# One list of steps for five engines, drawn in another order

## The chip, the core and the metric

The kernel runs on one core of a Trainium2 chip. The metric is device time in microseconds; the median of three runs before the change is 268.47 us (265.78 to 269.16). A profile of one execution goes with it.

## The reference

Four batches of 256 tokens of width 256 go through two layers. Layer 0 is attention and an MLP, each with a layer norm whose scale and shift, and a gate (gamma), come from a condition vector. Layer 1 is RMS norm and attention with rotary positions and a mask.

```python
def layer0(x, cond):                      # 16 heads of 16
    gamma1, gamma2, scale1, scale2, shift1, shift2 = split(silu(cond) @ Wada.T + bada)
    q, k, v = heads((ln(x) * (scale1 + 1) + shift1) @ Wqkv.T + qkv_bias)
    p = softmax(q / |q| * sm @ (k / |k|).T + attn_bias)
    x = x + ((p @ v) @ Wproj.T + bproj) * gamma1
    h = gelu_tanh((ln(x) * (scale2 + 1) + shift2) @ Wfc1.T + bfc1)    # width 1024
    return x + (h @ Wfc2.T + bfc2) * gamma2

def layer1(x, cond):                      # 4 heads of 64
    h = rms_norm(x, cond @ norm_w.T + 1)
    q, k, v = heads(h @ qkv_w.T)
    q, k = rope(q * sqrt(scale) / |q|, k * sqrt(scale) / |k|)
    return (softmax(where(mask, q @ k.T, -1e30)) @ v) @ out_w.T + x
```

The projections take their operands in high and low halves, so each is made of three matmuls (L785, L786, L787) where one would do.

## The kernel before

The work is cut into 407 steps such as `qk0:2.1`: a name whose last digit is the layer where there are two, the batch, and within it a tile of 128 tokens or an index of heads. Everything stays on the chip after the loads. `ORDER` is one list of all steps, and PE, DVE, ACT and POOL each walk it: `walk` runs, step by step, the part that belongs to its own engine and skips the rest. So each engine's instructions stand in the order of the list, and no engine overtakes itself. Between engines semaphores wait for the producer of an operand. PE's results go to three PSUM banks in turn, numbered in the list's order; `claim` waits until the user of the bank's last content, three results earlier in the list, has emptied it. SP's loads and stores are a program of their own beside the list.

The steps that are spoken of below. In layer 0, for a batch b: `stats0`, `norm0` (DVE: xh, L1136), `normed0` (PE transposes, ACT makes xmt at L588), `split0` (DVE: xm_hi and xm_lo, L1145 and L1146), `qk0:b.t` (PE L785 to L787, DVE L1256), `unit0`, `hi0` and `lo0` (the normalised q and k in halves), `turnq0` and `turnk0` (PE transposes, ACT copies to qstk at L659 and to kstk at L672 and L673), `max0:b.i` (PE L838, DVE row maxima at L1153, eight per batch and two instructions each), `score0:b.i` (PE L863, ACT exponentials at L598), `value0` (PE L883), `out0`, `heads0` (ACT L605, L606), `heads0_lo` (DVE L1193), `proj0`. `gamma:b` spreads a batch's gate over the partitions (PE L949, ACT L640); `bias_count` (DVE L1223, L1224) looks at the attention bias; `split_wqkv0` and `split_w1` make the halves of weights (ACT L569 the high half, DVE L1105 or POOL L517 the low one). The MLP is `fc1`, `gelu`, `fc2`. In layer 1: `square1` (POOL L536), `rsums1` (DVE L1344), `rope` (DVE L1360 to L1369), `turn1` (PE transposes, ACT L739), `score1:b.t` (PE L1032, L1037), `max1` (DVE L1376), `exp1` (ACT L750), `diag1` (DVE L1382, L1387), `turnp1` (PE L1047, copies on ACT L763 and DVE L1400), `value1` (PE L1062), `heads1`, `heads1_lo` (DVE L1404), `proj1`.

Of the kernel before, what the change touches and what calls it, by code (L numbers as in the profile page):

```python
# [73 lines left out]


ORDER = [(name, *map(int, filter(None, rest.split(".")))) for name, _, rest in (word.partition(":") for word in """
const_sel silu const_v zeros:0 stats0:0 norm0:0 ada split_wqkv0 normed0:0 head_scales split0:0 stats0:1
const_stack square0:0.0 square0:0.1 stats0:2 norm0:1 root0:0 qk0:0.0 qk0:0.1 sums0:0 normed0:1 zeros:1 split0:1
norm0:2 ada_rest stats0:3 v0:0 v0:1 unit0:0.0 unit0:0.1 normed0:2 square0:1.0 qk0:1.0 square0:1.1 root0:1
lo0:0.0 lo0:0.1 qk0:1.1 hi0:0.0 hi0:0.1 bias_count sums0:1 square0:2.0 turnk0:0.0 turnq0:0.0 turnq0:0.1 flag  # L80
split0:2 turnk0:0.1 gamma_rows max0:0.0 v0:2 max0:0.1 norm0:3 gamma:0 gamma:1 gamma:2 gamma:3 hi0:1.0
square0:2.1 hi0:1.1 unit0:1.0 unit0:1.1 max0:0.2 lo0:1.0 lo0:1.1 qk0:2.0 qk0:2.1 max0:0.3 max0:0.4 max0:0.5
turnk0:1.0 normed0:3 sums0:2 max0:0.6 max0:0.7 neg0:0 turnq0:1.0 turnq0:1.1 split0:3 shift0:0 split_wproj
turnk0:1.1 unit0:2.0 unit0:2.1 qk0:3.0 qk0:3.1 max0:1.0 score0:0.0 score0:0.1 max0:1.1 hi0:2.0 score0:0.2
max0:1.2 score0:0.3 max0:1.3 mask hi0:2.1 lo0:2.0 value0:0.0 max0:1.4 score0:0.4 score0:0.5 lo0:2.1 take0:0.0
max0:1.5 value0:0.1 max0:1.6 score0:0.6 score0:0.7 root0:2 max0:1.7 neg0:1 turnq0:2.0 out0:0.0 turnq0:2.1
shift0:1 square0:3.0 sums0:3 turnk0:2.0 turnk0:2.1 value0:0.2 value0:0.3 take0:0.1 max0:2.0 score0:1.0 max0:2.1
score0:1.1 square0:3.1 max0:2.2 score0:1.2 score0:1.3 unit0:3.0 hi0:3.0 max0:2.3 value0:1.0 max0:2.4 score0:1.4
xbias0:0 score0:1.5 unit0:3.1 hi0:3.1 max0:2.5 out0:0.1 value0:1.1 max0:2.6 take0:1.0 score0:1.6 score0:1.7
lo0:3.0 heads0:0 take0:1.1 root0:3 max0:2.7 neg0:2 heads0_lo:0 value0:1.2 value0:1.3 shift0:2 lo0:3.1 turnk0:3.0  # L90
proj0:0 turnq0:3.0 turnq0:3.1 turnk0:3.1 stats1:0 out0:1.0 out0:1.1 score0:2.0 max0:3.0 score0:2.1 max0:3.1
heads0:1 max0:3.2 score0:2.2 max0:3.3 score0:2.3 max0:3.4 score0:2.4 max0:3.5 score0:2.5 xbias1:0 xbias0:1
xbias1:1 heads0_lo:1 max0:3.6 value0:2.0 norm1:0 value0:2.1 max0:3.7 neg0:3 take0:2.0 xbias0:2 score0:2.6
split_w1 v0:3 score0:2.7 shift0:3 proj0:1 stats1:1 value0:2.2 value0:2.3 take0:2.1 score0:3.0 score0:3.1
out0:2.0 out0:2.1 score0:3.2 heads0_lo:2 score0:3.3 heads0:2 value0:3.0 value0:3.1 normed1:0 take0:3.0 norm1:1
xbias1:2 score0:3.4 score0:3.5 proj0:2 stats1:2 score0:3.6 score0:3.7 split_w2 value0:3.2 value0:3.3 split1:0
take0:3.1 out0:3.0 normed1:1 out0:3.1 split1:1 heads0_lo:3 norm1:2 fc1:0.0 xbias0:3 xbias1:3 fc1:0.1 fc1:0.2
heads0:3 fc1:0.3 gelu:0.0 gelu:0.1 gelu:0.2 gelu:0.3 fc1:1.0 fc1:1.1 proj0:3 stats1:3 split1:2 normed1:2 fc1:1.2
fc1:1.3 norm1:3 gelu:1.0 gelu:1.1 gelu:1.2 split_wqkv1 split_wout1 fc2:0 stats2:0 normed1:3 square1:0.0
square1:0.1 norm2:0 gelu:1.3 fc1:2.0 cos:0.0 fc1:2.1 cos:0.1 gelu:2.0 split1:3 fc1:2.2 gelu:2.1 split2:0 fc1:2.3  # L100
normed2:0 gelu:2.2 gelu:2.3 fc2:1 stats2:1 qk1:0.0 qk1:0.1 rsums1:0 norm2:1 fc2:2 root1:0 fc1:3.0 stats2:2
fc1:3.1 gelu:3.0 gelu:3.1 norm2:2 normed2:1 fc1:3.2 split2:1 gelu:3.2 cos:1.0 fc1:3.3 gelu:3.3 rope:0.0 v1:0
rope:0.1 normed2:2 qk1:1.0 square1:1.0 square1:1.1 split2:2 fc2:3 stats2:3 rsums1:1 turn1:0.0 max1:0.0 max1:0.1
qk1:1.1 turn1:0.1 score1:0.0 score1:0.1 norm2:3 exp1:0.0 rope:1.0 rope:1.1 diag1:0.0 v1:1 rsums1:2 qk1:2.0 v1:2
diag1:0.1 qk1:2.1 turn1:1.0 turn1:1.1 max1:1.0 normed2:3 exp1:0.1 turnp1:0.0 score1:1.0 score1:1.1 split2:3
rope:2.0 cos:1.1 turnp1:0.1 exp1:1.0 rope:2.1 qk1:3.0 qk1:3.1 diag1:1.0 max1:1.1 value1:0 turn1:2.0 rsums1:3
diag1:1.1 turn1:2.1 heads1_lo:0 exp1:1.1 root1:1 square1:2.0 square1:2.1 cos:2.0 heads1:0 turnp1:1.0 cos:2.1
score1:2.0 max1:2.0 score1:2.1 max1:2.1 turnp1:1.1 rope:3.0 rope:3.1 diag1:2.0 v1:3 exp1:2.0 value1:1 turn1:3.0
exp1:2.1 proj1:0 diag1:2.1 turn1:3.1 turnp1:2.0 turnp1:2.1 root1:2 heads1:1 heads1_lo:1 square1:3.0 max1:3.0
max1:3.1 diag1:3.0 score1:3.0 score1:3.1 square1:3.1 cos:3.0 value1:2 diag1:3.1 exp1:3.0 exp1:3.1 proj1:1  # L110
heads1_lo:2 heads1:2 turnp1:3.0 turnp1:3.1 root1:3 heads1_lo:3 proj1:2 value1:3 proj1:3 cos:3.1 heads1:3
""".split())]
# [1345 lines left out]
```

How the kernel before makes its waits and increments, by code:

```python
            def step(ins):  # L346
                count[0] += 1
                ins.then_inc(s, 1)
                eng.wait_ge(s, count[0])
# [8 lines left out]
        @block.sync  # L359
# [30 lines left out]
            sp.dma_start(mask_u8, mask.rearrange("b (t p) k -> p b t k", p=P)).then_inc(s_mask, 16)  # L390
            def shift_rows(b):
                sp.wait_ge(*emptied(("shT", b)))
                for par in range(2):
                    sp.dma_start(qstk[SLOT * par + 48:SLOT * par + 50, b % 2, :, :].bitcast(F32),
                                 shs[2 * PAIRS * par:2 * PAIRS * (par + 1), :]).then_inc(shift_in, 16)
            shift_rows(0)
            sp.wait_ge(*full(("gam_rows",)))
            sp.wait_ge(*emptied(("ada2",)))
            sp.dma_start(stage_a[:, 0:FC * HID].rearrange("p (f n) -> p f n", f=FC),
                         wfc1.rearrange("(f p) n -> p f n", p=P)).then_inc(s_w1, 16)
            sp.wait_ge(w_hi, 2)
            sp.wait_ge(w_lo_d, 2)
            sp.dma_start(stage_b[:, :].rearrange("p (f n) -> p f n", f=HC),
                         wfc2.rearrange("(f p) n -> p f n", p=P)).then_inc(s_w2, 16)
            for b in range(1, B):
                shift_rows(b)
            sp.wait_ge(w_hi, 3)
            sp.wait_ge(w_lo_p, 1)
            sp.dma_start(stage_a[:, 0:FC * 3 * C].rearrange("p (f n) -> p f n", f=FC),
                         wqkv1.rearrange("(f p) n -> p f n", p=P)).then_inc(s_wq1, 16)
            sp.wait_ge(w_hi, 4)
            sp.wait_ge(w_lo_p, 2)
```

## Time and profile before

| | before |
|---|---|
| median of 3 runs, us | 268.47 (265.78 to 269.16) |
| profiled execution, span, us | 266.0 |
| PE busy, us | 232.5 (87%) |
| DVE busy, us | 202.7 (76%) |
| ACT busy, us | 154.9 (58%) |
| POOL busy, us | 117.4 (44%) |
| mean granted clock of TensorE | 0.987 |

The profiled execution's own time is its span, 266.0 us from the first to the last instruction; it is 2.5 us shorter than the median of the runs. Seen by stage, 0 to 143 us is layer 0's attention, 143 to 199 the MLP, and 199 to 266 layer 1. A row of a timeline gives the start, the length, the engine and line, what is written from what, the number of instructions joined in it, and in brackets how long the engine stood idle ahead of it and what ended that.

### The profile page before, as it was taken

To read this page: it belongs to the slowest core of one execution; us is meant where nothing else is said; L and a number is where in the kernel's file an instruction comes from. 1 tells how busy PE (TensorE), PEld (TensorE's weight loads), DVE (VectorE), ACT (ScalarE), POOL (GpSimd) and SP (SyncE) were. 2 spreads that over 40 slices of the span, in tenths; PEclk is the share of its full clock that TensorE was granted. 3 is DMA by queue.
4 is the path that set the end of the run, shared out by engine and by line. 5 is a ranking of instruction groups with operands and counts; after the bars stand their busy time and mean duration, and the time that the engine had idled before them with its cause. 6 is when DMAs were issued, how large, how long until landed. Compare 5 with 4: busy or idle time off the path is not lost.

```text
span 266.0 us, 4823 instructions
## 1 busy us (share of the span) xinstructions
PE 232.5 (87%) x1710; PEld 186.4 (70%) x1710; DVE 202.7 (76%) x421; ACT 154.9 (58%) x303; POOL 117.4 (44%) x184
## 2 busy tenths in 40 slices
...
DMA packets 8248, 10.11 MB, mean 38 GB/s; under 512 B 1824, under 2 KB 7072, under 8 KB 8224
## 3 DMA queue, kind: packets, MB, share of 16 engines
...
q8 instruction: 15, 0.25, 0.4%
q14 instruction: 9, 0.07, 0.1%
...
## 4 chain that ended last, share of the span: by engine, by line
PE 51%; DVE 16%; ACT 11%; issue 8%; POOL 7%; DMA 3%; SPq 2%; ACTq 0%; DVEq 0%; POOLq 0%
PE ring L785 8%; PE ring L786 7%; PE ring L787 7%; PE ring L791 6%; PE ring L838 5%; PE psx L863 5%; PE pv L883 4%; DMA xs<-in_x 3%; PE ring L1047 3%; DVE nm L1153 3%; ACT kstk L673 3%; ACT kstk L672 2%; PE pv L1062 2%; ACT ps L598 2%; POOL nt L450 1%
## 5 line engine op out<-in xcount | busy, mean ns | idle before, releaser
L1153 DVE TENSOR_REDUCE nm<-ring 128x2 f32<-128x512 f32 x64 | 40.2, 683 | 5.3 <-PE ring L838 5.2
L598 ACT ACTIVATE ps<-psx 128x1024 f32<-128x1024 f32 x32 | 31.3, 1026 | 7.5 <-PE psx L863 4.3
L838 PE MATMUL ring<-kstk,qstk 128*128 128x512 f32 x64 | 25.0, 449 | 4.1 <-ACT kstk L673 2.7
L785 PE MATMUL ring<-wqkv_hi,xm_hi 128*128 128x512 f32 (+1 forms) x64 | 24.3, 379 | 4.4 <-DVE xm_lo L1146 2.9
L786 PE MATMUL ring<-wqkv_lo,xm_hi 128*128 128x512 f32 (+1 forms) x64 | 23.3, 364 | 0.0
L787 PE MATMUL ring<-wqkv_hi,xm_lo 128*128 128x512 f32 (+1 forms) x64 | 22.9, 358 | 0.0
L838 PEld LDWEIGHTS ring<-kstk,qstk 128*128 128x128 f32 x64 | 11.3, 193 | 13.9 <-DVE nm L1153 5.3
L791 PE MATMUL ring<-ident,stack 128*128 128x128 f32 x128 | 17.7, 278 | 2.9 <-ACT kstk L673 1.4
L863 PE MATMUL psx<-qstk,kstk 128*128 128x256 f32 x128 | 19.7, 287 | 0.3 <-ACT ps L598 0.3
L863 PEld LDWEIGHTS psx<-qstk,kstk 128*128 128x128 f32 x128 | 17.8, 189 | 2.5 <-ACT ps L598 0.9
L883 PE MATMUL pv<-ps,vs 128*32 128x256 f32 x256 | 16.1, 383 | 3.6 <-issue 3.3
L441 POOL TENSOR_TENSOR rstd<-ve,half_neg 128x2 f32<-128x2 f32 x12 | 9.3, 775 | 21.4 <-DVE ve L1122 20.3
L791 PEld LDWEIGHTS ring<-ident,stack 128*128 128x128 f32 x128 | 13.7, 141 | 7.0 <-issue 4.2
L785 PE MATMUL ring<-xm_hi,kstk 128*128 128x256 f32 x64 | 18.5, 289 | 0.1
L702 ACT ACTIVATE ps<-ring,col 128x256 f32<-128x256 f32 x32 | 13.2, 474 | 9.0 <-PE ring L787 8.8
L785 PEld LDWEIGHTS ring<-wqkv_hi,xm_hi 128*128 128x128 f32 x64 | 13.1, 205 | 7.6 <-issue 5.7
L588 ACT ACTIVATE xmt<-ring,mod 128x256 f32<-128x256 f32 x16 | 8.2, 561 | 17.5 <-PE ring L791 17.5
L750 ACT ACTIVATE ps<-psx,nm 128x256 f32<-128x256 f32 x32 | 14.7, 484 | 6.2 <-DVE nm L1376 6.2
L787 PE MATMUL ring<-xm_hi,kstk 128*128 128x256 f32 x64 | 18.1, 283 | 0.0
L786 PE MATMUL ring<-xm_lo,kstk 128*128 128x256 f32 x64 | 18.1, 283 | 0.0
L536 POOL TENSOR_TENSOR qn<-qk 128x512 f32<-128x512 f32 x8 | 9.1, 1142 | 20.0 <-ACT qk L724 15.2
L488 POOL TENSOR_TENSOR qn<-qk 128x512 f32<-128x512 f32 x8 | 8.3, 1042 | 20.9 <-DVE qk L1256 10.7
...
## 6 DMA issues: line engine op xcount, KB each, us to landing
...
```

Of the source, the lines that this page charges most:

```text
L441: g.tensor_tensor(rstd[:, kind, b, :], ve[:, kind, b, :], half_neg[:, 0:TB], ALU.pow)\
L598: a.activation(ps[:, n % 4], psx[:, n % 2], ACT.Exp).then_inc(exp_done, 1)
L702: last = a.activation(gelu_u[:, n % 4, i * L:(i + 1) * L], bank(key)[:, i * L:(i + 1) * L], ACT.Gelu_apprx_tanh, bias=col[:, 16 + 2 * i_ + ...
L750: ins = a.activation(weights_q[m % 2][:, i, f, :], psx[:, n % 2, i, f, :], ACT.Exp, bias=nm1[:, m % 2, 2 * i + f:2 * i + f + 1], accum_out ...
L785: mm(dst, lhs[0], rhs[0], start=start, stop=False)
L786: mm(dst, lhs[0], rhs[1], start=False, stop=False)
L787: return mm(dst, lhs[1], rhs[0], start=False, stop=stop)
L791: last = nc.tensor.transpose(dst[:, i * P:(i + 1) * P], src, ident[:, :])
L838: last = mm(dst, qstk[:, b % 2, p, qc * P:(qc + 1) * P], kstk[:, b % 2, 2 * p:2 * p + 2, :], start=True, stop=not with_bias)
L863: last = mm(dst[:, i, kc, :], kstk[:, b % 2, 2 * p + i, keys], qstk[:, b % 2, p, :], start=True, stop=not with_bias)
L883: last = mm(pv[32 * i:32 * i + 32, cols_], vs[:, b % 3, kc, 4 * g + i, :], ps[:, slot, i % 2, kc, :], start=(kc == 0), stop=(kc == TB - 1))
L1153: v.tensor_reduce(nm[:, qc, :, p], bank(key).rearrange("p (h n) -> p h n", h=2), AX.X, ALU.max, negate=True).then_inc(ring_dve, 1)
```

## The change

Only `ORDER` is redrawn. It holds the same 407 steps, with the same instructions, buffers, waits and loads; what differs is where each step stands, and with it which result gets which PSUM bank. The diff replaces all lines of the list; the lines of the two places with a shift on DVE below are these.

```diff
@@ -74,41 +74,42 @@
-const_sel silu const_v zeros:0 stats0:0 norm0:0 ada split_wqkv0 normed0:0 head_scales split0:0 stats0:1
-const_stack square0:0.0 square0:0.1 stats0:2 norm0:1 root0:0 qk0:0.0 qk0:0.1 sums0:0 normed0:1 zeros:1 split0:1
...
-diag1:0.1 qk1:2.1 turn1:1.0 turn1:1.1 max1:1.0 normed2:3 exp1:0.1 turnp1:0.0 score1:1.0 score1:1.1 split2:3
-rope:2.0 cos:1.1 turnp1:0.1 exp1:1.0 rope:2.1 qk1:3.0 qk1:3.1 diag1:1.0 max1:1.1 value1:0 turn1:2.0 rsums1:3
-diag1:1.1 turn1:2.1 heads1_lo:0 exp1:1.1 root1:1 square1:2.0 square1:2.1 cos:2.0 heads1:0 turnp1:1.0 cos:2.1
...
+const_sel const_v zeros:0 silu stats0:0 split_wqkv0 norm0:0 head_scales ada const_stack split0:0 stats0:1
+normed0:0 square0:0.0 qk0:0.0 square0:0.1 stats0:2 norm0:1 qk0:0.1 root0:0 sums0:0 normed0:1 split0:1 ada_rest
...
+root1:2 cos:2.1 split2:3 max1:1.0 max1:1.1 normed2:3 score1:1.0 score1:1.1 turnp1:0.0 turnp1:0.1 rope:2.0
+rope:2.1 exp1:1.0 exp1:1.1 diag1:1.0 rsums1:3 max1:2.0 diag1:1.1 qk1:3.0 qk1:3.1 value1:0 max1:2.1 turn1:2.0
+turn1:2.1 score1:2.0 score1:2.1 heads1:0 heads1_lo:0 turnp1:1.0 turnp1:1.1 exp1:2.0 exp1:2.1 rope:3.0 v1:3
...
```

The first place is DVE near the start: `split_wqkv0` (wqkv_lo) and `norm0:0` (xh). Before:

```order
L1122 TENSOR_SCALAR ve<-mv 128x2
L1136 TENSOR_SCALAR xh<-xs,mv,rstd 128x256 x2
L1092 TENSOR_TENSOR mod<-ring,col 128x8 x2
L1100 TENSOR_SCALAR mod<-mod 128x8
L1105 TENSOR_TENSOR wqkv_lo<-stage_b,wqkv_hi 128x1536
L1213 TENSOR_SCALAR sm<-row 128x16
L1145 CAST xm_hi<-xmt 128x512
L1146 TENSOR_TENSOR xm_lo<-xmt,xm_hi 128x512
```

and in the changed list:

```order
L1123 TENSOR_SCALAR ve<-mv 128x2
L1106 TENSOR_TENSOR wqkv_lo<-stage_b,wqkv_hi 128x1536
L1137 TENSOR_SCALAR xh<-xs,mv,rstd 128x256 x2
L1214 TENSOR_SCALAR sm<-row 128x16
L1093 TENSOR_TENSOR mod<-ring,col 128x8 x2
L1101 TENSOR_SCALAR mod<-mod 128x8
L1146 CAST xm_hi<-xmt 128x512
L1147 TENSOR_TENSOR xm_lo<-xmt,xm_hi 128x512
```

The low half of wqkv now stands ahead of xh. (Line numbers of the changed kernel are higher by one.)

The second place is ACT between batch 1's and batch 2's exponentials. kstk is written in `turnk0`, qstk in `turnq0`, o_raw in `take0`. Before:

```order
L673 ACTIVATE kstk<-ring 64x4x128
L618 ACTIVATE o_raw<-pv 128x512
L598 ACTIVATE ps<-psx 128x1024 x4
L649 ACTIVATE stack<-qn 128x32x16
L650 ACTIVATE stack<-qn 128x16x16
L651 ACTIVATE stack<-qn 128x16x16
L598 ACTIVATE ps<-psx 128x1024 x2
```

and in the changed list, where gam is `gamma:3`:

```order
L674 ACTIVATE kstk<-ring 64x4x128
L660 ACTIVATE qstk<-ring 128x4x128 x4
L619 ACTIVATE o_raw<-pv 128x512
L599 ACTIVATE ps<-psx 128x1024 x3
L641 ACTIVATE gam<-ring 128x512
L599 ACTIVATE ps<-psx 128x1024
L650 ACTIVATE stack<-qn 128x32x16
L651 ACTIVATE stack<-qn 128x16x16
L652 ACTIVATE stack<-qn 128x16x16
```

The copies of q now follow those of k, where they stood ahead of them, and the gate of batch 3 is spread between two exponentials of batch 2.

The third place is DVE in layer 1, from the rope of batch 2's second tile on; nm is `max1`, ss is `rsums1:3`, inv and o_raw are `diag1:1.0`. Before:

```order
L1400 COPY ps<-ring 128x4x128
L1360 TENSOR_TENSOR stage_a<-qk,rope_sb 128x512
L1365 TENSOR_TENSOR qn<-stage_a 128x8x32
L1366 TENSOR_TENSOR qn<-stage_a 128x8x32
L1369 TENSOR_TENSOR qn<-qn,rn 128x512
L1382 RECIPROCAL inv<-sums 128x4
L1387 TENSOR_TENSOR o_raw<-ident,inv 128x512
L1376 TENSOR_REDUCE nm<-psx 128x4
L1344 TENSOR_REDUCE ss<-qn 128x8 x2
L1348 TENSOR_SCALAR ss<-ss 128x2x8
L1112 TENSOR_SCALAR nt<-ss 128x2x8
L1113 TENSOR_SCALAR rn<-nt 128x2x8
```

and in the changed list:

```order
L1361 TENSOR_TENSOR stage_a<-qk,rope_sb 128x512
L1366 TENSOR_TENSOR qn<-stage_a 128x8x32
L1367 TENSOR_TENSOR qn<-stage_a 128x8x32
L1370 TENSOR_TENSOR qn<-qn,rn 128x512
L1383 RECIPROCAL inv<-sums 128x4
L1388 TENSOR_TENSOR o_raw<-ident,inv 128x512
L1345 TENSOR_REDUCE ss<-qn 128x8 x2
L1349 TENSOR_SCALAR ss<-ss 128x2x8
L1113 TENSOR_SCALAR nt<-ss 128x2x8
L1114 TENSOR_SCALAR rn<-nt 128x2x8
L1377 TENSOR_REDUCE nm<-psx 128x4
```

The maximum that stood between the diagonal and the sums of squares is gone from there (it stands ahead of the ropes of batch 2), and the next maximum comes after the sums.

Four more moves are spoken of. On PE, `score1:3.0` comes directly behind `turn1:3.1`, where `turnp1:2.0` and `turnp1:2.1` stood between; `qk0:2.0` and `qk0:2.1` come ahead of `max0:0.0`; the four `gamma` steps, which stood in a row, are spread from `max0:0.5` to `score0:1.2`. On POOL `split_w1` comes ahead of `xbias0:2` (L504, L505), which it followed. On ACT `normed1:0` comes ahead of batch 3's first exponential.

## Rows read from the trace of the kernel before

**Rows 1.** Windows: length, busy us of PE, PEld, DVE, ACT, POOL; granted clock; DMA.

```profile
46.00:53.00 7.00, 7.00 (x18) 4.93 (x17) 4.39 (x9) 3.56 (x9) 1.04 (x1) 0.51 0.00 0
...
143.00:199.00 56.00, 55.91 (x453) 54.97 (x452) 42.40 (x87) 32.86 (x69) 23.18 (x29) 1.00 0.02 6
199.00:266.00 67.00, 58.69 (x424) 45.16 (x422) 52.21 (x92) 32.36 (x95) 25.03 (x51) 1.00 0.05 17
```

**Rows 2.** Timeline of DVE at the start.

```profile
10.47 0.74 DVE L1136 TENSOR_SCALAR xh<-xs,mv,rstd 128x256 f32<-128x256 f32 x2 [4.43 <-POOL rstd L441]
...
11.94 1.75 DVE L1105 TENSOR_TENSOR wqkv_lo<-stage_b,wqkv_hi 128x1536 fp32r<-128x1536 f32 x1
...
13.69 0.41 DVE L1145 CAST xm_hi<-xmt 128x512 fp32r<-128x512 f32 x1
...
16.24 0.89 DVE L1118 BATCH_NORM_STATS2 bnst<-xs 128x6 f32<-128x256 f32 x2 [1.41 <-DMA xs<-in_x]
```

**Rows 3.** Timeline of ACT and PE at the start.

```profile
9.71 1.48 ACT L569 ACTIVATE wqkv_hi<-stage_b 128x1536 fp32r<-128x1536 f32 x1 [6.91 <-DMA stage_b<-in_wqkv]
12.42 1.02 ACT L588 ACTIVATE xmt<-ring,mod 128x256 f32<-128x256 f32 x2 [1.23 <-PE ring L791]
...
14.97 0.77 PE L785 MATMUL ring<-wqkv_hi,xm_hi 128*128 128x512 f32 x1 [2.60 <-DVE xm_lo L1146]
```

**Rows 4.** Groups of instructions: busy us, mean ns of one, idle before and its releasers.

```profile
L1153 DVE TENSOR_REDUCE nm<-ring 128x2 f32<-128x512 f32 x64 | 40.2, 683 | 5.3 <-PE ring L838 5.2
L598 ACT ACTIVATE ps<-psx 128x1024 f32<-128x1024 f32 x32 | 31.3, 1026 | 7.5 <-PE psx L863 4.3
```

**Rows 5.** DVE, PE and ACT from 33 to 54 us, with the window before the clock's fall.

```profile
33.86 0.69 DVE L1224 TENSOR_SCALAR_CACHE_REDUCE o_raw<-bias_sb 128x512 f32<-128x512 f32 x1
...
46.28 0.62 PE L949 MATMUL ring<-at_lo,sel 8*128 8x512 f32 x1
...
46.94 0.60 ACT L640 ACTIVATE gam<-ring 128x512 f32<-128x512 f32 x1 [0.24 <-PE ring L949]
...
50.66 0.69 DVE L1256 TENSOR_TENSOR qk<-ring,row 128x512 f32<-128x512 f32 x1 [0.36 <-PE ring L787]
53.10 0.69 DVE L1256 TENSOR_TENSOR qk<-ring,row 128x512 f32<-128x512 f32 x1 [1.75 <-PE ring L787]
...
44.00:46.00 2.00, 1.82 (x7) 1.14 (x8) 2.00 (x6) 1.09 (x2) 0.00 (x0) 0.99 0.00 0
```

**Rows 6.** DVE at the turn from batch 1 to batch 2.

```profile
87.81 3.68 DVE L1153 TENSOR_REDUCE nm<-ring 128x2 f32<-128x512 f32 x6 [3.86 <-PE ring L838]
```

**Rows 7.** ACT, DVE and POOL from 117 to 134 us; last, at_lo's durations (min/median/max).

```profile
117.94 1.94 ACT L598 ACTIVATE ps<-psx 128x1024 f32<-128x1024 f32 x2 [3.03 <-PE pv L883]
...
131.22 2.46 DVE L1193 TENSOR_TENSOR at_lo<-stage_a,at_hi 128x512 fp32r<-128x512 f32 x1 [2.22 <-ACT at_hi L606]
...
128.56 4.57 POOL L517 TENSOR_TENSOR kstk<-stage_a,kstk 128x2048 fp32r<-128x2048 f32 x1
...
L1193 DVE TENSOR_TENSOR at_lo<-stage_a,at_hi x4: 679/692/2460, 100.5 to 149.7; 128x512 fp32r<-128x512 f32 x4
```

**Rows 8.** PE before and at the start of the MLP.

```profile
133.82 0.36 PE L785 MATMUL ring<-wp_hi,at_hi 128*128 128x256 f32 x1 [0.65 <-DVE at_lo L1193]
...
143.26 0.36 PE L785 MATMUL ring<-xm_hi,kstk 128*128 128x256 f32 x1
```

**Rows 9.** DVE and POOL in layer 1, around the sums of batch 3.

```profile
227.85 1.22 DVE L1376 TENSOR_REDUCE nm<-psx 128x4 f32<-128x1024 f32 x1
...
229.99 0.69 DVE L1344 TENSOR_REDUCE ss<-qn 128x8 f32<-128x512 f32 x1 [0.31 <-POOL qn L536]
...
227.83 2.04 POOL L536 TENSOR_TENSOR qn<-qk 128x512 f32<-128x512 f32 x2 [4.23 <-ACT qk L724]
```

**Rows 10.** ACT and PE behind the last turn of layer 1.

```profile
242.18 0.62 ACT L739 ACTIVATE vs<-ring 128x512 f32<-128x512 f32 x1
...
242.12 3.81 PE L1047 MATMUL ring<-o_raw,ps 128*128 128x128 f32 x32
```

More of the change, by code:

```diff
@@ L76 @@
 ORDER = [(name, *map(int, filter(None, rest.split(".")))) for name, _, rest in (word.partition(":") for word in """
-const_sel silu const_v zeros:0 stats0:0 norm0:0 ada split_wqkv0 normed0:0 head_scales split0:0 stats0:1
-const_stack square0:0.0 square0:0.1 stats0:2 norm0:1 root0:0 qk0:0.0 qk0:0.1 sums0:0 normed0:1 zeros:1 split0:1
-norm0:2 ada_rest stats0:3 v0:0 v0:1 unit0:0.0 unit0:0.1 normed0:2 square0:1.0 qk0:1.0 square0:1.1 root0:1
-lo0:0.0 lo0:0.1 qk0:1.1 hi0:0.0 hi0:0.1 bias_count sums0:1 square0:2.0 turnk0:0.0 turnq0:0.0 turnq0:0.1 flag
@@ L81 @@
[L81 to L104, printed above, removed]
-diag1:0.1 qk1:2.1 turn1:1.0 turn1:1.1 max1:1.0 normed2:3 exp1:0.1 turnp1:0.0 score1:1.0 score1:1.1 split2:3
@@ L106 @@
-rope:2.0 cos:1.1 turnp1:0.1 exp1:1.0 rope:2.1 qk1:3.0 qk1:3.1 diag1:1.0 max1:1.1 value1:0 turn1:2.0 rsums1:3
-diag1:1.1 turn1:2.1 heads1_lo:0 exp1:1.1 root1:1 square1:2.0 square1:2.1 cos:2.0 heads1:0 turnp1:1.0 cos:2.1
-score1:2.0 max1:2.0 score1:2.1 max1:2.1 turnp1:1.1 rope:3.0 rope:3.1 diag1:2.0 v1:3 exp1:2.0 value1:1 turn1:3.0
-exp1:2.1 proj1:0 diag1:2.1 turn1:3.1 turnp1:2.0 turnp1:2.1 root1:2 heads1:1 heads1_lo:1 square1:3.0 max1:3.0
-max1:3.1 diag1:3.0 score1:3.0 score1:3.1 square1:3.1 cos:3.0 value1:2 diag1:3.1 exp1:3.0 exp1:3.1 proj1:1
@@ L111 @@
-heads1_lo:2 heads1:2 turnp1:3.0 turnp1:3.1 root1:3 heads1_lo:3 proj1:2 value1:3 proj1:3 cos:3.1 heads1:3
+const_sel const_v zeros:0 silu stats0:0 split_wqkv0 norm0:0 head_scales ada const_stack split0:0 stats0:1
+normed0:0 square0:0.0 qk0:0.0 square0:0.1 stats0:2 norm0:1 qk0:0.1 root0:0 sums0:0 normed0:1 split0:1 ada_rest
+norm0:2 stats0:3 v0:0 bias_count v0:1 unit0:0.0 unit0:0.1 normed0:2 qk0:1.0 square0:1.0 square0:1.1 root0:1
+lo0:0.0 square0:2.0 qk0:1.1 lo0:0.1 hi0:0.0 hi0:0.1 turnk0:0.0 zeros:1 sums0:1 turnq0:0.0 turnq0:0.1 norm0:3
@@ new lines @@
+flag split0:2 turnk0:0.1 gamma_rows v0:2 unit0:1.0 unit0:1.1 normed0:3 qk0:2.0 square0:2.1 lo0:1.0 qk0:2.1
+max0:0.0 max0:0.1 hi0:1.0 hi0:1.1 max0:0.2 max0:0.3 lo0:1.1 turnk0:1.0 sums0:2 turnk0:1.1 root0:2 max0:0.4
+max0:0.5 gamma:0 max0:0.6 max0:0.7 unit0:2.0 square0:3.0 mask turnq0:1.0 turnq0:1.1 square0:3.1 gamma:1 neg0:0
+unit0:2.1 hi0:2.0 shift0:0 max0:1.0 gamma:2 hi0:2.1 max0:1.1 max0:1.2 xbias0:0 score0:0.0 max0:1.3 score0:0.1
+max0:1.4 score0:0.2 score0:0.3 value0:0.0 split0:3 max0:1.5 score0:0.4 score0:0.5 lo0:2.0 max0:1.6 value0:0.1
```

24 lines of the change are left out of this document (added).

## The prediction

> **What bounds the kernel now.** I read three views. First the windows by stage, because each stage has its own limit [rows 1]. In the MLP (143 to 199 us) PE is busy 55.91 of 56.00 us: only an earlier or later start can move that stage. In layer 1 (199 to 266) no engine is full, PE 58.69 and DVE 52.21 of 67; the attention of layer 0 ahead of the MLP is of the same kind. What sets the time there is the order, since an engine that waits holds everything behind it. Second, the instructions one by one where the list differs; third, group rows for durations [rows 4].
>
> No instruction is added or removed, so the sum is made of waits alone: those of before that the new order fills, and those that it opens. I followed the new list engine by engine with the durations of before and noted how much later the same instruction comes. Terms that overlap don't add up, so each term below is the change of one running delay. The delay counts at two points: the first fc1 matmul, before at 143.26 [rows 8], since PE is full from there on, and the last scores.
>
> **1. Start, +2.3.** Before, DVE makes xh as soon as rstd is there (10.47, 0.74 long) and splits wqkv (11.94, 1.75) while PE transposes xh and ACT makes xmt (12.42, 1.02) [rows 2, 3]. Now the split stands ahead of xh. It needs ACT's high half, which runs from 9.71 to 11.19 [rows 3], so it ends near 11.19 + 1.75 = 12.94, and xh near 13.7, where it ended at 11.21. From xh's end to xmt's end it took 2.23 (11.21 to 13.44), from the cast's start to the first qk product 1.28 (13.69 to 14.97) [rows 2, 3]: 13.7 + 2.23 + 1.28 = 17.2 to 17.3 with a handover, +2.3. The floor is zero if something later waits for a DMA anyway: the statistics of batch 1 waited for their x till 16.24 [rows 2]. But they feed batch 1, and the first product leads the chain of batch 0, so I take the full 2.3.
>
> **2. 18 to 56 us, running +1.0.** On DVE bias_count (a reduction of 0.69 [rows 5] and a shorter instruction) is moved ahead of batch 0's values and of batch 1's second qk tile: +0.8. Against it: PE's granted clock was 0.51, the 1.2 GHz level, from 46 to 53 us [rows 1]. It fell as PE ran the four gamma steps in a row (the last matmul at 46.28, 0.62 long), and DVE then waited 0.36 and 1.75 us for qk0:2.0 and qk0:2.1 at half pace, 2.1 in the middle of its row of maxima [rows 5]. The new list spreads the gammas over the next stages and runs qk0:2.x ahead of the maxima. I take it that the clock stays up, and the 2.1 comes back: 2.3 + 0.8 - 2.1 = 1.0. The Trainium skill (TensorE: Matmul & The Clock Gate, "What's actually happening") lets the clock fall after the array has idled. The trace doesn't bear that out, for PE was busy 1.82 of the 2.00 us up to the fall [rows 5]; so I go by what ran. By the page, spreading the gammas would save nothing of itself, and the sum would be 2.1 higher.
>
> **3. Batches 1 to 3, 56 to 111 us, running +2.1.** The pace is DVE's 64 maxima of 0.683 us with ACT's 32 exponentials of 1.026 beside them [rows 4]. At the turn to batch 2 DVE waits 3.86 us for ACT's copies of k, ahead of the maxima [rows 6]. The new order puts q's copies behind k's; the maxima need both, so the same copies stand in line and the wait stays, less 0.1. Then gamma:3 (0.60 [rows 5]) is put between exponentials where ACT has no gap, and proj0:0 (twelve matmuls; such a step's first is at 133.82 [rows 8]) ahead of the k turn of batch 3: +1.2 together. Bounds: 0 if ACT's other waits swallow them, and about 2.3 (twice my value) if they also push a row of maxima.
>
> **4. 111 to 143 us, running +1.85.** value0:2.0 is taken earlier, which fills ACT's wait of 3.03 us at 117.94 [rows 7]; but the maxima on DVE go on meanwhile, so I count none of it. heads0_lo:2 took 2.46 us where the other three take 0.68 to 0.69; it ended at 133.68, 0.55 after POOL's 4.57 us split of w1 (128.56 to 133.13) [rows 7], and PE's projection waited for it [rows 8]. Now the split stands further ahead of it, by two POOL instructions that it followed: -1.8 at most, -1.2 after what PE does next. The other way, on ACT normed1:0 (two instructions, 1.02 as at 12.42 [rows 3]) comes ahead of score0:3.0, of which I count +0.7, and handovers +0.25. 2.1 + 0.7 + 0.25 - 1.2 = 1.85. The Trainium skill (SBUF — State Buffer, "Who interferes with whom") says that a DVE instruction with two SBUF inputs is held by a POOL instruction that reads SBUF until that one ends. The two ends, 0.55 us apart, agree. By the rule the gain hangs on POOL's split ending first; if it doesn't, the sum is 1.2 higher.
>
> **5. MLP, +0.15.** PE is full [rows 1], so the delay passes through. The second normalisation of batch 0 and some gelu steps change places: between 0 and 0.3.
>
> **6. Layer 1, +2.0.** (a) Before, max1:1.1 (1.22 at 227.85) filled DVE's time while POOL squared batch 3's q and k (2.04 from 227.83), and rsums1:3 waited only 0.31 [rows 9]. That maximum now stands ahead of the ropes of batch 2, and nothing fills: between 0 and 1.22, I take 0.75. (b) score1:3.0 now directly follows turn1:3.1 on PE, whose result ACT first copies (0.62 from 242.18); before, PE could start turnp1:2 at 242.12 and work on for 3.81 us [rows 10]. PE idles until 242.8 and a handover: between 0.7 and 0.9, I take 0.9. (c) score1:1.1 is ahead of turnp1:0.x, which delays qk1:3.x; mostly hidden under the ropes, 0.35 (bounds 0 and 1.22, its maximum's length). Sum 2.0, bounds 0 (the fillers replace one another) and 3.3. The tail from the last scores keeps its order.
>
> **Sum**: 1.85 + 0.15 + 2.0 = +4.0 us on a profiled span of 266.0. That execution lies near the fast end of the three runs, 2.5 under their median; 266.0 + 4.0 = 270.0 and 268.47 + 4.0 = 272.5. I forecast 271.5, nearer the second.
>
> **Rivals.** *The clock falls again* (chance 0.22). For it: batch 2's products still lie near 45 to 50 us, now ahead of all maxima, where nothing covers them. Against: the gammas are spread. Then the 2.1 isn't regained: 268.47 + 4.0 + 2.1 = 274.6, slower. *The filled waits are real gains* (0.14), the case on the other side. Mechanism: ACT, not DVE, paces 111 to 143, so the 3.03 at 117.94 comes off the MLP's start in full, and the stretched instruction's 1.8 too (0.6 more than counted). It decides if the last exponentials of batch 2 then follow one another without a gap. With it 4.0 - 3.0 - 0.6 = +0.4; with the 2.0 of layer 1 absorbed by the 8.3 us that PE is idle there, -1.6; and if the new order of copies also hides the 3.86, -5.5: 263 to 269. *The delays are absorbed* (0.24): the 2.3 of the start dies at the first wait that doesn't hang on batch 0, and layer 1's fillers replace each other: 0 to +1.5, 268.5 to 270. That the list isn't what runs is excluded: all engines walk it.
>
> **Numbers.** My forecast has the remaining 0.40 and the range 269.5 to 274 of its own. 2% of 268.47, about what a measurement of this kernel can tell from no change, is 5.4: faster is below 263.1, slower above 273.8. Faster 0.13: the far end of the gains' case (0.07), and 0.06 for waits that such a walk doesn't see. Slower 0.35: most of the clock's case (0.18), a fifth of my own (0.08), 0.09 for the upper bounds of terms 3 and 6. Within: 0.52. The range of 264.5 to 276.5 leaves out only the far end of the gains, and the clock's fall together with upper bounds.
>
> **What would show it.** Right: first qk product at 17.3; no fall of the clock before the maxima; fc1 near 145.1; a wait over 1 us ahead of rsums1:3; PE idle ahead of score1:3.0. Wrong: fc1 at or before 143.3, or from fc1 to the end no longer than the 122.7 us of before.

## The result and the profile after

The changed kernel takes 276.64 us (median of 4 runs, 275.61 to 278.42), the kernel before beside it 268.63; the ratio is 1.0325 (95% interval 1.0278 to 1.0373): 8 us slower, where 3 were forecast and 276.5 was the end of the range. The profiled span is 273.7 us against 266.0, +7.7. That execution took 275.61 by the clock of the runs, so some 1.9 us lie around the span.

The same instruction's start, before and after, shows where the 7.7 come from. All are starts on PE.

| | before | after | late by |
|---|---|---|---|
| first qk product | 14.97 | 17.38 | 2.41 |
| shift0:0 | 63.44 | 66.63 | 3.19 |
| max0:2.0 | 87.23 | 89.94 | 2.71 |
| max0:3.0 | 108.83 | 112.11 | 3.28 |
| score0:3.0 | 125.64 | 128.70 | 3.06 |
| score0:3.7, the last score | 135.80 | 137.45 | 1.65 |
| fc1:0.0 | 143.26 | 148.74 | 5.48 |
| fc2:3 | 193.22 | 198.97 | 5.75 |
| proj1:3 | 261.02 | 268.77 | 7.75 |

So 1.65 had been lost at the last scores, 3.83 more went between them and fc1, 0.27 in the MLP and 2.00 in layer 1. The biggest piece lies in a stretch of 8 us to which the prediction gave nothing.

The start first, DVE and PE after (columns as in [rows 2, 3]):

```profile
11.39 1.76 DVE L1106 TENSOR_TENSOR wqkv_lo<-stage_b,wqkv_hi 128x1536 fp32r<-128x1536 f32 x1 [5.35 <-ACT wqkv_hi L570]
13.07 0.73 DVE L1137 TENSOR_SCALAR xh<-xs,mv,rstd 128x256 f32<-128x256 f32 x2
```

```profile
17.38 0.77 PE L786 MATMUL ring<-wqkv_hi,xm_hi 128*128 128x512 f32 x1 [2.41 <-DVE xm_lo L1147]
```

The split runs when its high half is there, xh follows it, and the first product comes at 17.38, as worked out from [rows 2, 3].

Where [rows 5] had DVE wait for qk0:2.x at half clock, the changed kernel has the clock down later. PE there, in the middle of batch 0's maxima, and two windows (columns as in [rows 1], the granted clock third from the end):

```profile
57.38 0.50 PE L839 MATMUL ring<-kstk,qstk 128*128 128x512 f32 x1 [0.72 <-ACT kstk L674]
58.60 1.22 PE L839 MATMUL ring<-kstk,qstk 128*128 128x512 f32 x2 [0.72 <-ACT kstk L674]
```

```profile
56.00:58.00 2.00, 1.00 (x2) 0.37 (x2) 1.50 (x6) 1.93 (x5) 0.83 (x3) 1.00 0.00 0
...
60.00:62.00 2.00, 2.00 (x5) 1.03 (x5) 0.99 (x3) 0.60 (x1) 1.46 (x5) 0.50 0.00 0
```

PE was busy half of the time (1.00 of 2.00 us) before it fell. The delay, 3.19 at shift0:0, is about halved by the last scores, in part because PE no longer waits 0.65 [rows 8] for heads0_lo:2, 0.69 us where [rows 7] had 2.46:

```profile
134.31 0.69 DVE L1194 TENSOR_TENSOR at_lo<-stage_a,at_hi 128x512 fp32r<-128x512 f32 x1 [2.87 <-ACT at_hi L607]
```

Now PE around the last scores. First the kernel before, which the rows ahead of the prediction did not show here, then the changed one:

```profile
135.32 1.12 PE L863 MATMUL psx<-qstk,kstk 128*128 128x256 f32 x8
139.77 1.93 PE L883 MATMUL pv<-ps,vs 128*32 128x256 f32 x32 [3.33 <-issue]
141.64 0.66 PE L791 MATMUL ring<-ident,o_raw 128*128 128x128 f32 x4
```

```profile
136.97 1.12 PE L864 MATMUL psx<-qstk,kstk 128*128 128x256 f32 x8
140.90 1.93 PE L884 MATMUL pv<-ps,vs 128*32 128x256 f32 x14 [2.81 <-issue]
144.00 1.01 PE L884 MATMUL pv<-ps,vs 128*32 128x256 f32 x2 [1.17 <-issue]
144.94 1.12 PE L792 MATMUL ring<-ident,o_raw 128*128 128x128 f32 x4
145.99 1.55 PE L884 MATMUL pv<-ps,vs 128*32 128x256 f32 x16
```

"issue" is time for which the profile shows no wait. Before, PE stands once for 3.33 us and then does 32 matmuls in 1.93. After, it stands for 2.81, does 14, and stands again for 1.17; around this second stop it works at half pace, for the 14 take the 1.93 that 32 took. The windows after show the clock:

```profile
138.00:140.00 2.00, 0.09 (x1) 0.00 (x0) 1.86 (x5) 1.59 (x2) 1.20 (x1) 1.00 0.09 31
140.00:142.00 2.00, 1.10 (x11) 0.68 (x15) 1.22 (x4) 0.00 (x0) 1.69 (x4) 0.55 0.03 8
142.00:144.00 2.00, 0.83 (x7) 0.00 (x0) 0.00 (x0) 0.00 (x0) 1.21 (x1) 0.50 0.00 0
144.00:146.00 2.00, 2.00 (x8) 0.86 (x8) 0.00 (x0) 0.00 (x0) 0.00 (x0) 0.50 0.00 0
146.00:148.00 2.00, 2.00 (x21) 1.00 (x20) 0.75 (x3) 0.39 (x1) 0.00 (x0) 0.75 0.00 0
```

It falls to 0.50, the 1.2 GHz level, while PE stands, and comes back at 147. Before, the same window views from 136 to 144 read 1.00 throughout, though its one stop was longer than either of these. What is at this place in the code: PE alone has two branches on a flag (attention bias zero or not) from the first maximum to the last score. The first is taken, the second jumped over, and both meet behind the last score.

```python
with nc.tensor.If(bias_flag == 0):
    walk(ORDER[FIRST_SCORE:AFTER_SCORES], False)
with nc.tensor.If(bias_flag != 0):
    walk(ORDER[FIRST_SCORE:AFTER_SCORES], True)
walk(ORDER[AFTER_SCORES:], False)
```

Last, layer 1 after: the sums of batch 3 (DVE), and PE ahead of score1:3.0.

```profile
235.49 0.69 DVE L1345 TENSOR_REDUCE ss<-qn 128x8 f32<-128x512 f32 x1 [1.01 <-POOL qn L537]
236.49 0.69 DVE L1345 TENSOR_REDUCE ss<-qn 128x8 f32<-128x512 f32 x1 [0.31 <-POOL qn L537]
```

```profile
249.76 0.59 PE L1033 MATMUL psx<-mask_add,ident_b 128*128 128x512 bf16 x2 [0.73 <-issue]
```

Both waits that the prediction named are there, 1.01 + 0.31 where [rows 9] had 0.31, and 0.73.

### The profile page after: what moved, and what is told of

It reads as the page before. It is cut to its first block, busy times and chain, and to the rows that moved or that the text cites. A ratio compares the mean times of both kernels' runs of the same rounds, so it can differ in the third digit from the quotient of the medians.

```text
span 273.7 us, 4822 instructions
## 1 busy us (share of the span) xinstructions
PE 237.8 (87%) x1710; PEld 188.4 (69%) x1710; DVE 208.3 (76%) x421; ACT 154.4 (56%) x303; POOL 115.5 (42%) x184
## 4 chain that ended last, share of the span: by engine, by line
PE 61%; DVE 13%; ACT 11%; issue 6%; DMA 4%; POOL 2%; SPq 1%; ACTq 0%; DVEq 0%
PE ring L786 8%; PE ring L788 8%; PE ring L787 8%; PE ring L792 7%; PE pv L884 6%; PE ring L839 6%; PE ring L1048 6%; PE psx L864 5%; PE pv L1063 3%; DMA stage_b<-in_wqkv 3%; ACT ps L599 3%; ACT kstk L673 2%; ACT kstk L674 2%; PE psx L1038 2%; DMA qstk<-stage_a 2%
## 5 line engine op out<-in xcount | busy, mean ns | idle before, releaser
L839 PE MATMUL ring<-kstk,qstk 128*128 128x512 f32 x64 | 26.9, 479 | 3.1 <-ACT kstk L674 2.0
L884 PE MATMUL pv<-ps,vs 128*32 128x256 f32 x256 | 18.9, 408 | 4.0 <-issue 4.0
L864 PE MATMUL psx<-qstk,kstk 128*128 128x256 f32 x128 | 20.4, 289 | 1.1 <-ACT ps L599 0.5
L792 PE MATMUL ring<-ident,stack 128*128 128x128 f32 x128 | 18.7, 298 | 2.9 <-ACT kstk L674 1.6
L792 PEld LDWEIGHTS ring<-ident,stack 128*128 128x128 f32 x128 | 15.8, 155 | 5.8 <-issue 4.0
```

Source lines behind the costliest of these rows:

```text
L792: last = nc.tensor.transpose(dst[:, i * P:(i + 1) * P], src, ident[:, :])
L839: last = mm(dst, qstk[:, b % 2, p, qc * P:(qc + 1) * P], kstk[:, b % 2, 2 * p:2 * p + 2, :], start=True, stop=not with_bias)
L864: last = mm(dst[:, i, kc, :], kstk[:, b % 2, 2 * p + i, keys], qstk[:, b % 2, p, :], start=True, stop=not with_bias)
L884: last = mm(pv[32 * i:32 * i + 32, cols_], vs[:, b % 3, kc, 4 * g + i, :], ps[:, slot, i % 2, kc, :], start=(kc == 0), stop=(kc == TB - 1))
```

## The experiments

Two theories for the 3.83 us. **A**: they are PE's stall where the branches meet, and the clock's fall in it. **B**: the new order of the steps behind the last scores waits for something that the profile shows as issue. The runs are e1 to e13; "one branch" means that both branches reach to the end of the program.

**e1 and e2: the branches meet behind everything.** The same edit on the list of before (e1) and on the changed one (e2):

```diff
 with nc.tensor.If(bias_flag == 0):
-    walk(ORDER[FIRST_SCORE:AFTER_SCORES], False)
+    walk(ORDER[FIRST_SCORE:], False)
 with nc.tensor.If(bias_flag != 0):
-    walk(ORDER[FIRST_SCORE:AFTER_SCORES], True)
-walk(ORDER[AFTER_SCORES:], False)
+    walk(ORDER[FIRST_SCORE:], True)
```

> List of before; PE's two branches on the bias flag reach to the end of the program, so they meet behind PE's last instruction and not behind the last scores. Theory A (what was lost between the last scores and fc1 is PE's stall where the branches meet, with the clock that falls in it): the 3.33 us gap at 136.44 is gone, value0:3.2 follows the exponentials (137.94), fc1 starts near 141.4, about 1.9 earlier, and the span is near 264. Theory B (the new order of the steps behind the last scores is what costs): the gap is a wait that shows as issue, and nothing changes: span 266 +- 0.7.

> The changed list with the same edit. Theory A: the gaps of 2.81 and 1.17 and the half clock from 140.2 to 147.1 are gone; fc1, 10.65 us behind the end of score0:3.7 in the changed kernel, comes about 5 behind it; 273.7 goes to about 268, and what is left against before with the same edit is the 1.65 of the attention and the 2.0 of layer 1, about 3.7. Theory B: the changed kernel keeps fc1 at +3.8 against before; 273.7 +- 1.

Measured: e1 265.92 us (span 264.0), ratio to before 0.9905 (0.9876 to 0.9935); e2 269.54 (span 267.5), 1.0047 (1.0018 to 1.0077). PE in e2, the same place:

```profile
136.87 1.12 PE L864 MATMUL psx<-qstk,kstk 128*128 128x256 f32 x8
137.92 1.07 PE L884 MATMUL pv<-ps,vs 128*32 128x256 f32 x16
138.92 0.66 PE L792 MATMUL ring<-ident,o_raw 128*128 128x128 f32 x4
139.54 1.07 PE L884 MATMUL pv<-ps,vs 128*32 128x256 f32 x16
```

The stops are gone and the clock stays up there. From the last score's start to fc1 it takes 4.95 in e1 and 4.67 in e2 (7.46 before, 11.29 after): the new order is, if anything, the shorter one there. B falls. The meeting point costs 2.5 us with the list of before and 6.6 with the changed one; without it the lists differ by 3.6 us instead of 8.

**e3: one step of the start moved back.**

```diff
-... stats0:0 split_wqkv0 norm0:0 head_scales ada const_stack ...
+... stats0:0 norm0:0 head_scales ada split_wqkv0 const_stack ...
```

> The changed list with one step moved back: split_wqkv0 stands behind norm0:0 and ada again. My account: the first qk product comes 2.4 us earlier, at 15.0; rival: that is lost again before the first maxima, or the clock's falls shift, and the end moves by less than 1. By my running delay (1.65 at the last scores, of which 2.4 came from the start) the end comes 1 to 2.4 earlier: 271.3 to 272.7.

275.18 us (span 272.0), in the median 1.5 under the changed kernel, though the runs overlap (273.67 to 278.96 against 275.61 to 278.42). But the edit did not do what it was meant to: the first qk product is at 16.80, not 15.0. ACT shows why.

```profile
12.21 0.22 ACT L630 ACTIVATE sm<-sm 128x16 f32<-128x16 f32 x1 [9.46 <-DVE sm L1214]
12.33 1.47 ACT L570 ACTIVATE wqkv_hi<-stage_b 128x1536 fp32r<-128x1536 f32 x1
```

The high half now stands behind head_scales, which waits through DVE for a load (rows land at 12.0). One delay took the place of the other; e7 does it properly.

**e4: layer 1 in the order of before.** Behind fc2:3 both lists hold the same 97 steps, so that part can be exchanged whole.

```diff
 <changed list up to fc2:3>
-<97 steps, changed order>
+<97 steps, order of before>
```

> The changed list up to fc2:3, and behind it the 97 steps of layer 1 in the order of before (the same steps stand there in both lists). My account: fc2:3 stays 5.7 late and the 2.0 us that layer 1 added are gone: from fc2:3's start to the end 72.8 as before, in place of 74.7; the span is 271.7. Rival (the delay of layer 1 came from the state in which it is entered, not from its order): still 74.7.

275.09 us, in the median 1.5 under the changed kernel; here too the runs overlap (273.11 to 276.51). The stage says it more sharply than the total: from fc2:3 to proj1:3 67.79 us (201.59 to 269.38), in before 67.80, in the changed kernel 69.80. My expectation counted to the program's end; the difference is the same 2.0. The span itself was 274.3, since the meeting point cost more in this execution (12.32 from the last score to fc1).

**e5 and e6: the code shifted, nothing executed changed.** The changed kernel's second stop came behind exactly 14 matmuls. The moved steps qk0:2.x, v0:2 and normed0:3 stand ahead of the branches now, once in the code and not twice, so the meeting point lies some 60 PE instructions earlier by my count. Padding the branch that is not taken moves it. (That 120 of these waits make 60 instructions, and 392 make 196, is my count too.)

```diff
 with nc.tensor.If(bias_flag != 0):
+    for _ in range(120):          # e5, changed list: 60 instructions; e6, list of before: range(392), 196
+        pe.wait_ge(const_ready, 1)
     walk(ORDER[FIRST_SCORE:AFTER_SCORES], True)
```

> The changed list; the branch that PE doesn't take is made 60 instructions longer, nothing that is executed changes. In the changed kernel PE stopped a second time (1.17 us) 14 matmuls behind the point where the branches meet, in before it did not. Theory A1 (the second stop is the fetch of the next block of instructions, and where it lies depends on where the meeting point lies in its block; by my count the changed list moves that point by 60 instructions, since qk0:2.x, v0:2 and normed0:3 now stand once ahead of the branches instead of in both): the stop behind 14 matmuls is gone, as in before; -1.2, and the half clock that followed shortens too: fc1 comes 2 to 4 us earlier, span 270 to 272. Rival A2 (the order behind the scores, value0:3.2, out0:3.0, value0:3.3, makes the stop): it stays behind 14 matmuls, 273.7.

> The list of before; the branch not taken is made 196 instructions longer, which by the same count puts the meeting point where the changed list has it. A1: a second stop of about 1.2 appears some 14 matmuls behind it, and the clock may fall there; fc1 1.2 to 4 later, span 267 to 270. A2: nothing changes, 266.0 +- 0.7.

PE in e5, then in e6:

```profile
136.94 1.12 PE L864 MATMUL psx<-qstk,kstk 128*128 128x256 f32 x8
141.30 1.93 PE L884 MATMUL pv<-ps,vs 128*32 128x256 f32 x16 [3.23 <-issue]
143.16 1.12 PE L792 MATMUL ring<-ident,o_raw 128*128 128x128 f32 x4
```

```profile
133.89 1.12 PE L863 MATMUL psx<-qstk,kstk 128*128 128x256 f32 x8
138.21 1.06 PE L883 MATMUL pv<-ps,vs 128*32 128x256 f32 x14 [3.21 <-issue]
141.41 2.72 PE L883 MATMUL pv<-ps,vs 128*32 128x256 f32 x18 [2.14 <-issue]
```

The second stop has gone from the one and come to the other, behind 14 matmuls again. e3 and e4, whose edits leave the meeting point where the changed list has it, stop a second time behind 14 too (0.90 and 1.44 us). So its place hangs on where the code lies and not on what is executed, as A1 has it.

That PE fetches code there can be read from the traces, in their DMA packets of the kind "instruction", 16 KiB each (times in us):

| | PE stops | packet | PE goes on | next packet | PE stops again |
|---|---|---|---|---|---|
| before | 136.44 | 137.09 to 138.07 | 139.77 | 140.32 to 141.39 | no |
| after | 138.09 | 138.24 to 139.31 | 140.90 | 141.46 to 142.51 | 142.83 to 144.00 |
| e5 | 138.07 | 138.19 to 139.59 | 141.30 | 141.85 to 142.91 | no |
| e6 | 135.00 | 135.57 to 136.63 | 138.21 | 138.77 to 140.10 | 139.27 to 141.41 |

One packet starts within 0.7 us of the beginning of each first stop, the next some 0.55 us behind its end; PE goes on 1.3 to 1.7 us after a packet has landed. Where PE stops again, its work had run out before the second packet landed (e6) or 0.3 us behind that (after). In e1 and e2 no such packet moves between the last scores and fc1. That these packets are PE's, and that the work between the stops is the rest of the first one, is inferred from these times.

e6 takes 271.96 us, ratio to before 1.0143 (1.0106 to 1.0179): before's own list loses 3.5 us by code that never runs. From the last score to fc1 it takes 4.60 longer, 2.14 of it the second stop and the rest with the clock, which stayed up in the first stop and fell at 139.5, in the second. (This execution reached the last score 1.4 earlier than the profiled one of before.) The six runs of e5 lie between 270.6 and 275.3; the ratio to before is 1.0150 (1.0089 to 1.0211), where the changed kernel's was 1.0325, so the stop's going is a gain. The profiled one (span 273.4, expected were 270 to 272) had the clock down from 140 to 147 all the same. Its mean granted clock is 0.956, that of the two fastest runs 0.980 and 0.981: by that difference they had some 13 us less at the half clock (an estimate), in which places isn't shown.

The Trainium skill (Runtime: NRT & Kernel Launch, "Instruction fetch mechanics") says that code is fetched ahead in sequence only, in blocks of 256 instructions, and that a taken branch to a place that isn't at hand waits for its block. The rows agree: a stop and a packet behind each jump. That 196 instructions more bring in the stop that 60 fewer had brought fits blocks of that length too, for the two shifts differ by 256.

**e7 and e8: the start, then also layer 1, of before, on one branch.**

```diff
-... stats0:0 split_wqkv0 norm0:0 head_scales ada const_stack split0:0 stats0:1 normed0:0 ...
+... stats0:0 norm0:0 ada split_wqkv0 normed0:0 head_scales const_stack split0:0 stats0:1 ...   # e7; e8 also e4's edit
```

> The changed list with the branches that reach to the end, and the whole start of before: split_wqkv0 behind norm0:0 and ada, and head_scales behind normed0:0 (in the run with split_wqkv0 alone ACT's high half waited behind head_scales till 12.33). First qk product at 15.0 in place of 16.7. If the start's delay lives on to the end, 267.5 - 1.7 = 265.8; if it is absorbed before the MLP, 267.5 +- 0.5.

> The same with the 97 steps of layer 1 in the order of before. Layer 1's 2.0 are gone as in the run with layer 1 alone: 2.0 under the run before it, near 263.8 to 265.5. If it is under 264.0 it beats the kernel of before with the same branches, so the middle of the new list is a gain there.

e7 has its first product at 14.75 and takes 267.36 us (span 265.6), 2.2 less than e2: the start's delay lives on to the end. (2.0 of it stand in the trace: 16.73 to 14.75. The one run of each with the same high granted clock, 0.987, took 267.43 and 265.38, 2.05 apart.) e8 takes 265.12, another 2.2 less, ratio to before 0.9877 (0.9836 to 0.9918): it lies under both kernels (span 263.6, just under the 264.0 named). Against e1, the list of before with the same branches, it is 0.8 us ahead; the runs overlap (263.93 to 266.44 against 265.23 to 266.15), so the middle of the new list is no clear gain.

**e9: POOL's split earlier, on e1.** heads0_lo:2 took 2.47 us in e1 beside POOL's split of w1, 0.69 in the changed list, where the split ends just ahead of it.

```diff
-... xbias0:2 score0:2.6 split_w1 ... proj0:1 stats1:1 value0:2.2 ...
+... score0:2.6 split_w1 ... proj0:1 stats1:1 xbias0:2 value0:2.2 ...
```

> The list of before with the branches that reach to the end, and one step moved: xbias0:2 behind stats1:1, so that POOL's split of w1 (4.58, in that kernel from 128.99 to 133.57) starts some 2 us earlier and ends before heads0_lo:2. If that DVE instruction took 2.47 there because it had to wait for POOL's, it takes 0.69 now, the projection of batch 2 and fc1 come 1.2 to 1.8 earlier, 264.0 - 1.2 = 262.8 or less, median near 264.5. If its length has nothing to do with POOL, it stays at 2.47 and the time at 264.0.

270.36 us, 4.4 slower than e1, the opposite of both. heads0_lo:2 did come down to 0.69 us. But (DVE, then POOL):

```profile
126.64 4.56 DVE L1121 TENSOR_SCALAR ve<-mv 128x2 f32<-128x2 f32 x1
...
135.15 0.69 DVE L1192 TENSOR_TENSOR at_lo<-stage_a,at_hi 128x512 fp32r<-128x512 f32 x1 [2.38 <-ACT at_hi L606]
```

```profile
126.63 4.55 POOL L517 TENSOR_TENSOR kstk<-stage_a,kstk 128x2048 fp32r<-128x2048 f32 x1
```

An instruction on two elements per partition, 0.17 us elsewhere, took 4.56 and ended within 0.02 of POOL's split. Everything behind it on DVE waited, PE stood, and its clock fell to 0.50 from 132 to 138. So POOL's long instruction does hold DVE here, and not only instructions with two operands in SBUF. The changed kernel has such rows as well, in its MLP, where PE stayed busy. DVE, then POOL:

```profile
150.78 5.05 DVE L1137 TENSOR_SCALAR xh<-x,mv,rstd 128x256 f32<-128x256 f32 x2
```

```profile
151.06 4.62 POOL L522 TENSOR_TENSOR kstk<-stage_b,kstk 128x2048 fp32r<-128x2048 f32 x1 [7.85 <-ACT kstk L570]
```

Such a pair took 0.73 at the start (13.07 above). Moving POOL's split chooses which DVE instruction is hit: in e9 a costly one, in the changed kernel none beside split_w1 (129.69 to 134.27) and this one beside split_w2. The Trainium skill (SBUF — State Buffer, "Who interferes with whom") says that tensor_scalar, too, can need the ports that POOL holds, when its operands allow. These rows agree.

**e10 to e12: pieces of layer 1, on e7.**

```diff
-... max1:1.0 max1:1.1 ... diag1:1.0 rsums1:3 ... turn1:2.1 score1:2.0 ...      # e10 (exp1:1.1 moves too)
+... max1:1.0 ... diag1:1.0 max1:1.1 rsums1:3 ... turn1:2.1 exp1:1.1 score1:2.0 ...
-... heads1:1 score1:3.0 max1:3.0 cos:3.0 heads1_lo:1 turnp1:2.0 turnp1:2.1 max1:3.1 ...   # e11
+... heads1:1 cos:3.0 heads1_lo:1 turnp1:2.0 turnp1:2.1 score1:3.0 max1:3.0 max1:3.1 ...
-... score1:1.0 score1:1.1 turnp1:0.0 turnp1:0.1 ...                              # e12: e10 and this
+... turnp1:0.0 score1:1.0 score1:1.1 turnp1:0.1 ...
```

> The changed list with the start of before and the branches that reach to the end; in layer 1 max1:1.1 is put back behind diag1:1.0 (and exp1:1.1, which needs it, behind turn1:2.1). From fc2:3's start to proj1:3's it took 69.80 with the changed list where the clock didn't fall in it (before 67.80). My terms: the filled wait ahead of rsums1:3 is worth 0.75 of the 2.0: 69.0, and the wait ahead of rsums1:3 is at 0.3 again. Rival: all of the 2.0 hangs on it: 67.8.

> The same base; in layer 1 score1:3.0 is put back behind turnp1:2.1 and max1:3.0 ahead of max1:3.1. My term: 0.9 of the 2.0, so 68.9 from fc2:3's start to proj1:3's, and PE doesn't idle behind turn1:3.1. Rival: PE's 0.73 there is made up elsewhere, 69.8.

> The changed list with the start of before and the branches that reach to the end; in layer 1 max1:1.1 and exp1:1.1 are put back as in the run with the maximum alone, and turnp1:0.0 goes ahead of score1:1.0 on PE and DVE as in before. With the maximum alone nothing was gained: DVE waited 0.77 and 1.09 ahead of the two copies of turnp1:0 instead, since PE does score1:1.1 first. If these two moves belong together, the stretch from turn1:2.1 to score1:3.1 on PE comes down from 21.2 towards 19.8 and the one before it (fc2:3 to turn1:2.1) from 34.84 towards 34.3 where the clock stays up: some 1.2 in all. Rival: both stay, and what layer 1 lost hangs on later steps.

From turn1:2.1 to score1:3.1 on PE it took 19.84 us before, 21.22 after, 21.35 in e10, 20.85 in e11 and 22.11 in e12. So score1:3.0 is worth 0.4, and the maximum nothing: in e10 the wait ahead of the sums is back at 0.28, but DVE waits 0.77 and 1.09 for PE ahead of the two copies of turnp1:0. e12 removed the first of these and lost 0.9 further on. The whole stage from fc2:3 to proj1:3, which the expectations name, took 70.62 in e10, where the clock fell in it (211 to 215), 69.45 in e11 and 70.54 in e12. The medians (267.38, 266.94 and 266.92 against e7's 267.36) tell none of the three apart from e7. Only the whole order gives the 2.0 back (e4, e8).

**e13: the stop without its second half, 2 us earlier.** e7's list with the branches that meet behind the scores, and e5's padding.

> The changed list with the start of before, PE's branches meeting behind the last scores as in the changed kernel, and the branch not taken 60 instructions longer. The second stop is gone as in the run with the shift alone. If the clock falls in the first stop again (it did in every profile of the changed list, and not in before), fc1 comes some 9.5 to 10 behind score0:3.7's start: span 271; if it doesn't, 7.5: span 268.5. A spread of the runs of 2 to 4 us between these two says that the fall is a matter of the single execution.

272.23 us (270.64 to 273.60; span 269.8), 4.9 more than e7. The stop is 3.09 us, the only one; the clock falls at 139.7, 0.4 behind its end, and is back at 143, and fc1 comes 9.17 behind the last score's start, a little under the expected 9.5 to 10. The spread of the runs is 3.0 us (270.64 at a mean clock of 0.975, 273.60 at 0.950), within the 2 to 4 that the expectation took as a sign that the fall varies between executions. In the profiles, one stop with a fall costs 4.5 (9.17 against e2's 4.67; e5 has 5.3), one without a fall 2.5 (before against e1), and two with a fall 6.6 (after against e2).

| | stops, us | clock fell | last score to fc1, us |
|---|---|---|---|
| e2, changed list, one branch | none | no | 4.67 |
| before | 3.33 | no | 7.46 |
| e13 | 3.09 | yes | 9.17 |
| e5 | 3.23 | yes | 9.95 |
| after | 2.81, 1.17 | yes | 11.29 |
| e3 | 3.05, 0.90 | yes | 11.51 |
| e6, list of before | 3.21, 2.14 | yes, in the second | 12.06 |
| e4 | 2.83, 1.44 | yes | 12.32 |

What stays open: why the clock stayed up in the stop of 3.33 us before and in e6's of 3.21, and fell in or just behind the five shorter ones. One execution was profiled of each. The granted clock of the other runs says that executions differ: of the 17 of before beside e1, the six at 0.987, the profile's value, took 266.1 to 268.4 us, the eight at 0.974 or 0.968 took 268.2 to 269.4. Those spent some 7 to 10 us more at the half clock (an estimate from that difference); whether it was in the stop isn't shown.

## Why the prediction was wrong

**The step that failed** is one that was not taken. Between terms 4 and 5 the walk went from the last scores to fc1 at the durations of before, the 3.33 us stall of the kernel before included as it stood, and counted nothing for it. The list doesn't say how PE's code lies in memory, and I treated the order as the only thing that a new order changes. It also sets what stands ahead of the branches and what in both, and with that where they meet in the code. The runs show that the 3.83 us lie at this meeting point (without it the stretch takes 4.67 in e2 and 4.95 in e1), and that PE waits there for code. The shift of the meeting point, 60 instructions by my count, gave the second stop of 1.17 us, with the half clock around it worth 1.3 (11.29 against e5's 9.95) to 2.1 (against e13's 9.17). The rest, 1.7 to 2.5, is the clock's fall at the first stop, which the profiled execution of before didn't have; what decides on it stays open.

**Term by term.** Term 1, 2.3: measured 2.41, and e7 shows that it reaches the end. Term 2, running 1.0: 3.19 at shift0:0. The clock did not stay up; instead of once for 6.8 us it fell from 28 to 31, from 51 to 55 and from 58 to 65, the last time while PE did one or two matmuls at a time between waits of 0.52 to 0.72 us for ACT's copies. So spreading the gammas did not keep it up, and "I go by what ran" was one place read as a rule. Here PE was idle half of the time ahead of the fall; the Trainium skill (TensorE: Matmul & The Clock Gate, "What's actually happening"), which ties the fall to idleness, fits this place better than [rows 5]. It doesn't fit the first fall, at 27.55: PE was busy throughout from 24 to 27.5, the first 2.3 us of it on matmuls of 4 columns. Term 3, running 2.1: 3.28. Term 4, running 1.85: 1.65, near by luck: the loss in terms 2 and 3 was 1.2 larger, and 1.4 came back around batch 2's projection (3.06 at score0:3.0, 1.65 at score0:3.7). Of that, 0.65 is PE's wait for heads0_lo:2, which is gone; [rows 8] shows no more than this, so the term's 1.2 for it was too much. Most of the rest is eight transposes (out0:2.0 and normed1:0) that now stand ahead of score0:3.0. Term 5, 0.15: 0.27. Term 6, 2.0: 2.00 measured and 2.0 in e4. But of its parts only (b) was confirmed, at 0.4 and not 0.9; the filled wait (a) is real as a wait and worth nothing by itself. Its division was wrong, so the 2.0 was right as a sum by luck. The tail did not quite keep its order either: on PE proj1:1 and value1:2 change places, which cost 0.08 from score1:3.1 to proj1:3 (13.66 before, 13.74 after).

**The rivals.** "The clock falls again" was the nearest: same agent, a price of 2.1 and 274.6. Its place was wrong (near 45 to 50, while it fell from 51 on, and half of the delay was made up before the last scores); where it cost the end was in the stop behind the scores. "The filled waits are real gains" is refuted: ACT's 3.03 was filled (take0:2.0 came only 0.07 late, where max0:3.5 was 4.66 late) and the last scores still came 1.65 later. "The delays are absorbed" is refuted by e7 for the start and by e4 for layer 1.

**The base.** I took the span of 266.0 as 2.5 under the median. Part of that, some 1.9, is what lies around every span, so 272.5 was the consistent sum and 271.5 mixed two scales.
